# Row normalisation of three layer norms moved from VectorE to GpSimd in a one-core decoder layer

## The chip, the cores and the metric

One NeuronCore of a Trainium2 chip runs the whole kernel. The metric is the time of one execution on the device in microseconds (us); lower is better.

## What is computed

A decoder layer over 4 batches of 512 tokens with 512 columns: gated linear attention with 16 heads, attention on a context, and a feed-forward part with quantised weights and a Hadamard transform. Behind each of the three the result is added to the row and the row is normalised, without weight or bias:

```python
def _layernorm(x, axis=-1, eps=1e-05):
    m = jnp.mean(x, axis=axis, keepdims=True)
    v = jnp.var(x, axis=axis, keepdims=True)
    return (x - m) / jnp.sqrt(v + eps)

x = _layernorm(x + _L0_attn_ref(x, ...), axis=-1)
x = _layernorm(x + _L0_xattn_ref(x, ctx_1024, ...), axis=-1)
x = _layernorm(x + _L0_ffn_ref(x, ...), axis=-1)
```

All inputs and the output are fp32. The feed-forward part quantises each normalised row by its largest absolute value, to 8 bits.

## The kernel before

Y (128 partitions x 16 tiles x 512 columns) holds the rows of the layer all the time: tile 4b + i has the 128 tokens i of batch b. Attention goes in 32 steps, one for a pair of heads and a batch; each step adds its share into four tiles of Y (L1236). When a batch has had its last head pair, its cross part starts, and is spread between the stages of the following steps; behind the last step ("the seam") the feed-forward part goes in 64 units of 128 hidden columns, four of them to a batch tile of the down projection.

Every engine runs its own list of instructions in order and waits on semaphores (named in `S[...]`). The lists come from one order that all engines walk through: `attention_order`, `seam_order` and `ffn_order`. Between the stages of the steps, the table `PLACES` names for each batch at which place a stage of its cross part comes (for batch 0 `centre=400, n1=406, x101=414`, for batch 3 `centre=518, n1=520, x101=524`), and the table `UNIT` does the same for the stages of a unit (`add` 35 units behind the gate matmul, `normal` 37, `low` 2). An engine that has nothing to do at a stage passes it.

The three norms, before the change:

- First norm (`n1`), four tiles at a time. Stage `centre`: VectorE takes `bn_stats` (L1240), `bn_aggr` (L1242) and adds EPS to the variance (L1244) for each tile; GpSimd raises each to the power -1/2 (`root`, L1513). Stage `n1`: VectorE normalises four tiles (`normalise`, L1249). TensorE turns the tiles in stages `x101` and `x123` (L661).
- Second norm (`n2`), tile by tile. Stage `xm0_out` to `xm3_out`: VectorE first finishes the tile before (`finish`: normalise L1249, largest absolute value L1268), adds the product into Y (L1319) and takes the moments. GpSimd takes the root. The fourth tile is finished in `x_round1`.
- Third norm (`n3`), tile by tile in stages `add` (L1424 to L1431, for the last tile L1413 to L1420) and `normal` (L1434), the root on GpSimd (L1537). Then the tile is stored.

What else these engines do there. VectorE: masks of scores (L1194, L1146), the gate product GS (L1360), the product M of gate and up (L1367), the scaling of Wo slices (L1081), the scale of attention rows XI (L1257), the rounding of rows (L1340) and of hidden rows (L1402). GpSimd: the low parts of split fp32 weights (L1491), the clamp and cast of ternary weights (L1499, L1502), the root for the gated attention output (L1509), and LO, the low part of M (L1532). M has three buffers: its product n waits until LO of product n - 3 is written (`dve.wait_ge(S["h_lo"], n - 2)`, a count). TensorE's PSUM banks are handed on in the order of a table (`HOLD`): a matmul waits until the engine that reads its bank's last content is through. TensorE's lines: L486, L489, L492 the three passes of a split fp32 product, L549 scores, L600 weights, L614 values, L591 the turn of the exponentials, L646 energies, L719 gate and up, L728 the second Hadamard pass, which reads LO.

Of the kernel before, what the change touches and what calls it, by code (L numbers as in the profile page):

```python
# [10 lines left out]
ALU = mybir.AluOpType  # L11
# [7 lines left out]
EPS = 1e-5  # L19
# [221 lines left out]
def build(nc, x, xT, Wq, Wk, Wv, Wg, Ws, Wo, gw, cT, xWqT, xbq, xWkT, xbk, wgT, wuT, wdT, cst, out):  # L241
    with ExitStack() as top:
# [12 lines left out]
        Y = sb("Y", [128, 16, 512])  # L255
# [813 lines left out]
        def vector(engine):  # L1069
# [168 lines left out]
            def centre(name, k, i):  # L1238
# [4 lines left out]
                dve.wait_ge(S[name + "_moments"], 2 * k + 2)  # L1243
                engine.tensor_scalar(rs[:, i:i + 1], mv[:, i, 1:2], EPS, None, ALU.add).then_inc(S[name + "_var"], 1)  # L1244

            def normalise(name, k, i):
                y = Y[:, k, :]
                dve.wait_ge(S[name + "_rstd"], k + 1)
                engine.tensor_scalar(y, y, mv[:, i, 0:1], rs[:, i:i + 1], ALU.subtract,  # L1249
                                     ALU.mult).then_inc(S[name + "_applied"], 1)  # L1250
# [14 lines left out]
            def finish(b, i):  # L1265
                normalise("n2", 4 * b + i, i)
# [4 lines left out]
            def cross(stage, b):  # L1271
# [11 lines left out]
                elif stage == "n1":  # L1283
                    for i in range(4):
                        normalise("n1", 4 * b + i, i)
# [27 lines left out]
                elif stage in ("xm0_out", "xm1_out", "xm2_out", "xm3_out"):  # L1313
# [7 lines left out]
                    centre("n2", 4 * b + i, i)  # L1321
                elif stage in ("x_round0", "x_round1"):
# [30 lines left out]
            def ffn(stage, n):  # L1353
# [19 lines left out]
                elif stage in ("scale", "clamp", "turn_q_out", "add", "normal"):  # L1373
                    ffn_tile(stage, n)

            def ffn_tile(stage, i):
# [32 lines left out]
                elif stage == "add" and i == 15:  # L1409
# [7 lines left out]
                    dve.wait_ge(S["n3_moments"], 32)  # L1417
                    engine.bn_aggr(mv3[:, k, :], st3[:]).then_inc(S["n3_moments"], 1)
                    dve.wait_ge(S["n3_moments"], 33)
                    engine.tensor_scalar(rs3[:, k:k + 1], mv3[:, k, 1:2], EPS, None, ALU.add).then_inc(S["n3_var"], 1)  # L1420
                elif stage == "add":
# [6 lines left out]
                    dve.wait_ge(S["n3_moments"], 2 * i + 1)  # L1428
                    engine.bn_aggr(mv3[:, k, :], st3[:, k, :]).then_inc(S["n3_moments"], 1)
                    dve.wait_ge(S["n3_moments"], 2 * i + 2)  # L1430
                    engine.tensor_scalar(rs3[:, k:k + 1], mv3[:, k, 1:2], EPS, None, ALU.add).then_inc(S["n3_var"], 1)  # L1431
                elif stage == "normal":
                    dve.wait_ge(S["n3_rstd"], i + 1)
                    engine.tensor_scalar(y, y, mv3[:, k, 0:1], rs3[:, k:k + 1], ALU.subtract,  # L1434
                                         ALU.mult).then_inc(S["n3_applied"], 1)
# [44 lines left out]
        def gpsimd(engine):  # L1480
# [30 lines left out]
            def root(name, k, i):  # L1511
                pool.wait_ge(S[name + "_var"], k + 1)
                engine.tensor_tensor(rs[:, i:i + 1], rs[:, i:i + 1], half[:, 0:1], ALU.pow).then_inc(S[name + "_rstd"], 1)  # L1513

            def cross(stage, b):
# [4 lines left out]
                elif stage == "centre":  # L1520
                    for i in range(4):
                        root("n1", 4 * b + i, i)
# [227 lines left out]
```

## Time and profile before

| | us |
|---|---|
| three runs | 1487.88, 1489.14, 1489.43 |
| median | 1489.14 |
| the profiled execution | 1489.89 |
| its span, first to last instruction | 1488.1 |
| TensorE matmul busy in it | 1449.3 |
| VectorE busy | 1090.8 |
| ScalarE busy | 639.2 |
| GpSimd busy | 435.8 |

The engines are PE (TensorE, its weight loads PEld), DVE (VectorE), ACT (ScalarE), POOL (GpSimd) and SP (SyncE). A busy time says how long an engine worked, not whether anyone waited for it. The span is some 1.8 us shorter than the time of the same execution. A row in brackets `[1.57 <-DVE M L1367]` says that the engine stood idle for that long before the instruction, and which instruction ended the wait.

### The profile page before, as it was taken

The page shows a single profiled execution, that of the slowest core. Times are in us where ns is not written, and L with a number is a line of the kernel's source. Part 1 is how long each engine was busy: PE and PEld are TensorE (multiplying, and loading weights), DVE is VectorE, ACT ScalarE, POOL GpSimd, SP SyncE. Part 2 cuts the span into 40 slices and gives each one's busy share as a digit, 9 for nine tenths or more (in the row PEclk, how much of TensorE's full clock was granted, in tenths as well). Part 3 has the DMA queues.
Part 4 walks back from the last instruction along what each step waited for, and adds up shares of the span by engine and source line. Part 5 has one row for each costly group of instructions (what it writes and reads, how often), then busy time and mean ns, then how long its engine had stood idle before and what let it go on. Part 6 is the DMA issues. An engine that isn't in the chain of part 4 may idle for free.

```text
span 1488.1 us, 23933 instructions
## 1 busy us (share of the span) xinstructions
PE 1449.3 (97%) x9206; PEld 1170.7 (79%) x9240; DVE 1090.8 (73%) x2060; ACT 639.2 (43%) x1205; POOL 435.8 (29%) x282
## 2 busy tenths in 40 slices
PE   8999999999999999999999999999999898999998
PEld 6888888888888888888888888878888555666675
DVE  5567766676667777776677687687787786977788
ACT  4333333333323333333434334234343457776775
POOL 0311011211205455435454423221421343333320
PEclk9999999999999999999999999999999999999999
DMA  5545433443524454445655311101211125344552
GB/s 157 176 133 132 119 97 103 124 118 95 152 69 136 118 141 127 132 110 134 171 155 160 112 43 51 51 7 36 79 43 49 73 79 184 114 135 140 158 172 91
DMA packets 213297, 166.53 MB, mean 112 GB/s; under 512 B 89664, under 2 KB 174528, under 8 KB 213184
## 3 DMA queue, kind: packets, MB, share of 16 engines
q1 hardware_dynamic: 191920, 133.27, 30.5%
q10 hardware_dynamic: 21264, 31.73, 7.1%
q8 instruction: 74, 1.21, 0.4%
q14 instruction: 39, 0.32, 0.1%
HBM read 115.02 MB, written 49.94 MB: 111 GB/s over the span
## 4 chain that ended last, share of the span: by engine, by line
PE 86%; DVE 7%; DMA 2%; ACT 2%; POOL 2%; issue 1%; SPq 0%; POOLq 0%; ACTq 0%; DVEq 0%
PE bank L486 17%; PE bank L492 17%; PE bank L489 17%; PE bank L719 7%; PE bank L614 4%; PE bank L734 4%; PE bank L755 3%; PE bank L576 2%; PE bank L549 2%; PE bank L600 2%; DVE AM L1194 1%; PE bank L571 1%; PE bank L557 1%; PE bank L584 1%; DVE OKM L1172 1%
## 5 line engine op out<-in xcount | busy, mean ns | idle before, releaser
L486 PE MATMUL bank<-Wh,X 128*128 128x512 f32 x512 | 205.6, 402 | 0.1
L492 PE MATMUL bank<-Wh,X 128*128 128x512 f32 x512 | 200.0, 391 | 0.0
L489 PE MATMUL bank<-Wl,X 128*128 128x512 f32 x512 | 199.3, 389 | 0.0
L486 PE MATMUL bank<-X,Wh 128*128 128x512 f32 x384 | 156.7, 408 | 6.3 <-ACT Wh L812 6.3
L1491 POOL TENSOR_TENSOR Wl<-RAW,Wh 128x512 fp32r<-128x512 f32 (+1 forms) x65 | 112.1, 1735 | 136.8 <-ACT Wh L812 136.6
L492 PE MATMUL bank<-X,Wl 128*128 128x512 f32 x384 | 151.2, 394 | 0.0
L489 PE MATMUL bank<-X,Wh 128*128 128x512 f32 x384 | 150.6, 392 | 0.0
L1509 POOL TENSOR_TENSOR sm<-sm,half 128x8 f32<-128x8 f32 x32 | 52.7, 1648 | 331.9 <-DVE sm L1201 331.9
L1532 POOL TENSOR_TENSOR LO<-M,HI 128x512 fp32r<-128x512 f32 x64 | 82.7, 1292 | 161.7 <-PE bank L728 131.6
L874 ACT ACTIVATE V<-bank 128x256 f32<-128x256 f32 x128 | 49.0, 383 | 183.0 <-PE bank L492 182.8
L719 PE MATMUL bank<-XT,W 128*128 128x512 bf16 x492 | 119.3, 383 | 1.2 <-issue 0.2
L1499 POOL TENSOR_SCALAR RAW<-RAW 128x1024 f32<-128x1024 f32 x24 | 88.7, 3696 | 92.3 <-ACT RAW L835 90.2
L492 PEld LDWEIGHTS bank<-Wh,X 128*128 128x128 f32 x512 | 96.1, 188 | 20.9
L489 PEld LDWEIGHTS bank<-Wl,X 128*128 128x128 f32 x512 | 96.4, 188 | 18.0
L912 ACT ACTIVATE OG<-bank 128x512 f32<-128x512 f32 x64 | 38.3, 599 | 168.3 <-PE bank L614 168.3
L486 PEld LDWEIGHTS bank<-Wh,X 128*128 128x128 f32 x512 | 96.3, 188 | 18.0 <-ACT Kt L882 0.4
L1136 DVE RECIPROCAL ZT<-ZT 128x512 f32<-128x512 f32 x32 | 107.3, 3353 | 1.1
L486 PE MATMUL bank<-Woh,OTh 128*128 128x512 f32 x256 | 99.9, 390 | 0.0
L489 PE MATMUL bank<-Wol,OTh 128*128 128x512 f32 x256 | 99.6, 389 | 0.0
L492 PE MATMUL bank<-Woh,OTl 128*128 128x512 f32 x256 | 99.6, 389 | 0.0
L1172 DVE TENSOR_TENSOR OKM<-bank,ZT 128x512 f32<-128x512 f32 x32 | 22.1, 691 | 96.5 <-PE bank L576 96.4
L719 PEld LDWEIGHTS bank<-XT,W 128*128 128x128 bf16 x512 | 49.1, 99 | 53.4 <-issue 5.8
(219 smaller groups left out, 3282.0 us busy)
## 6 DMA issues: line engine op xcount, KB each, us to landing
z_scratch<-EV SPq DMA_DIRECT2D x64, 256.0 KB, 2.1
Z<-z_scratch SPq DMA_DIRECT2D x16, 1024.0 KB, 5.8
o_scratch<-OG ACTq DMA_DIRECT2D x96, 128.0 KB, 2.4
AM<-o_scratch ACTq DMA_DIRECT2D x24, 512.0 KB, 4.6
RAW<-wgT SPq DMA_DIRECT2D x16, 512.0 KB, 4.6
RAW<-wuT SPq DMA_DIRECT2D x16, 512.0 KB, 4.3
RAW<-wdT SPq DMA_DIRECT2D x16, 512.0 KB, 4.4
RAW<-Wo SPq DMA_DIRECT2D x14, 512.0 KB, 4.4
```

Source lines behind the costliest of these rows:

```text
L486: engine.matmul(o, lh(c), rh(c), start=c == 0, stop=False)
L489: engine.matmul(o, lh(c), rl(c), start=False, stop=False)
L492: last = engine.matmul(o, ll(c), rh(c), start=False, stop=c == n - 1)
L614: mm = engine.matmul(bo[h][:, 128 * i:128 * i + 128], AM[:, h, i, :], V[:, par, i, 128 * h:128 * h + 128], start=False, stop=i == 3)
L719: mm = engine.matmul(bk[:], w[:, c, 128 * j:128 * j + 128], XT[b % 3][:, c, :], start=c == 0, stop=c == 3)
L734: mm = engine.matmul(bh[:, 128 * c:128 * c + 128], Z[:, i % 2, 4 * q + c, :], C[:, 4, :], start=True, stop=True)
L874: engine.activation(V[:, par, i, :], bk[:, 0:256], ACT.Copy).then_inc(S["v_evac"], 1)
L1136: engine.reciprocal(ZT[:], ZT[:]).then_inc(S["z_recip"], 1)
L1491: engine.tensor_tensor(lo, r, hi, ALU.subtract).then_inc(S["w_lo_g"], 1)
L1499: engine.tensor_scalar(r, r, MAGIC - 1.0, MAGIC + 1.0, ALU.max, ALU.min).then_inc(S["w3_clip"], 1)
L1509: engine.tensor_tensor(smv[:, 4, :], smv[:, 3, :], half[:, 0:8], ALU.pow).then_inc(S["o_rstd"], 1)
L1532: engine.tensor_tensor(LO[:, n % 2, :], M[n % 3], HI[:, n % 3, :], ALU.subtract).then_inc(S["h_lo"], 1)
```

## The change

The normalise instruction goes to GpSimd's list for all three norms, with the same operands and at the same stage; for the second norm it follows the root of its tile at once. In the first norm VectorE adds EPS to the four variances of a batch in one instruction and GpSimd takes their four roots in one. In the third norm VectorE's `bn_aggr` waits until the normalise of the tile two before has been done, since it writes the same mean.

```diff
@@ vector @@
                 engine.bn_aggr(mv[:, i, :], st[:, i, :]).then_inc(S[name + "_moments"], 1)
-                dve.wait_ge(S[name + "_moments"], 2 * k + 2)
-                engine.tensor_scalar(rs[:, i:i + 1], mv[:, i, 1:2], EPS, None, ALU.add).then_inc(S[name + "_var"], 1)
-
-            def normalise(name, k, i):
-                y = Y[:, k, :]
-                dve.wait_ge(S[name + "_rstd"], k + 1)
-                engine.tensor_scalar(y, y, mv[:, i, 0:1], rs[:, i:i + 1], ALU.subtract,
-                                     ALU.mult).then_inc(S[name + "_applied"], 1)
+
+            def variances(name, k, i, tiles=1):
+                dve.wait_ge(S[name + "_moments"], 2 * (k + tiles))
+                engine.tensor_scalar(rs[:, i:i + tiles], mv[:, i:i + tiles, 1], EPS, None,
+                                     ALU.add).then_inc(S[name + "_var"], tiles)
             def finish(b, i):
-                normalise("n2", 4 * b + i, i)
                 dve.wait_ge(S["n2_applied"], 4 * b + i + 1)
                     for i in range(4):
                         centre("n1", 4 * b + i, i)
-                elif stage == "n1":
-                    for i in range(4):
-                        normalise("n1", 4 * b + i, i)
+                    variances("n1", 4 * b, 0, 4)
                     centre("n2", 4 * b + i, i)
+                    variances("n2", 4 * b + i, i)
                     dve.wait_ge(S["n3_moments"], 2 * i + 1)
+                    dve.wait_ge(S["n3_applied"], i - 1)
                     engine.bn_aggr(mv3[:, k, :], st3[:, k, :]).then_inc(S["n3_moments"], 1)
-                elif stage == "normal":
-                    dve.wait_ge(S["n3_rstd"], i + 1)
-                    engine.tensor_scalar(y, y, mv3[:, k, 0:1], rs3[:, k:k + 1], ALU.subtract,
-                                         ALU.mult).then_inc(S["n3_applied"], 1)
@@ gpsimd @@
-            def root(name, k, i):
-                pool.wait_ge(S[name + "_var"], k + 1)
-                engine.tensor_tensor(rs[:, i:i + 1], rs[:, i:i + 1], half[:, 0:1], ALU.pow).then_inc(S[name + "_rstd"], 1)
+            def root(name, k, i, tiles=1):
+
+                pool.wait_ge(S[name + "_var"], k + tiles)
+                engine.tensor_tensor(rs[:, i:i + tiles], rs[:, i:i + tiles], half[:, 0:tiles],
+                                     ALU.pow).then_inc(S[name + "_rstd"], tiles)
+
+            def normalise(name, k, i):
+                y = Y[:, k, :]
+                pool.wait_ge(S[name + "_rstd"], k + 1)
+                engine.tensor_scalar(y, y, mv[:, i, 0:1], rs[:, i:i + 1], ALU.subtract,
+                                     ALU.mult).then_inc(S[name + "_applied"], 1)
                 elif stage == "centre":
+                    root("n1", 4 * b, 0, 4)
+                elif stage == "n1":
                     for i in range(4):
-                        root("n1", 4 * b + i, i)
+                        normalise("n1", 4 * b + i, i)
                 elif stage in ("xm0_out", "xm1_out", "xm2_out", "xm3_out"):
                     root("n2", 4 * b + i, i)
+                    normalise("n2", 4 * b + i, i)
+                elif stage == "normal":
+                    y = Y[:, n, :]
+                    pool.wait_ge(S["n3_rstd"], n + 1)
+                    engine.tensor_scalar(y, y, mv3[:, k, 0:1], rs3[:, k:k + 1], ALU.subtract,
+                                         ALU.mult).then_inc(S["n3_applied"], 1)
```

The last tile's `bn_aggr` has the same new wait. Where the instructions come to stand on each engine, first on VectorE in the second norm of batch 0. Before:

```order
L1319 TENSOR_TENSOR Y<-Y,bank 128x512
L1240 BN_STATS st<-Y 128x6
L1242 BN_AGGR mv<-st 128x2
L1244 TENSOR_SCALAR rs<-mv 128x1
L1172 TENSOR_TENSOR OKM<-bank,ZT 128x512
L1249 TENSOR_SCALAR Y<-Y,mv,rs 128x512
L1268 TENSOR_REDUCE ax<-Y 128x1
L1319 TENSOR_TENSOR Y<-Y,bank 128x512
```

and now (L1313 is L1319, L1246 is L1244, L1264 is L1268):

```order
L1313 TENSOR_TENSOR Y<-Y,bank 128x512
L1240 BN_STATS st<-Y 128x6
L1242 BN_AGGR mv<-st 128x2
L1246 TENSOR_SCALAR rs<-mv 128x1
L1172 TENSOR_TENSOR OKM<-bank,ZT 128x512
L1264 TENSOR_REDUCE ax<-Y 128x1
L1313 TENSOR_TENSOR Y<-Y,bank 128x512
```

The normalise between the variance and the largest absolute value is gone from VectorE; everything else keeps its turn. On GpSimd, from the last root of attention on (the first norm of batch 3, in the feed-forward part; `sm` is the root L1509, `LO` the low part), before:

```order
L1509 TENSOR_TENSOR sm<-sm,half 128x8
L1532 TENSOR_TENSOR LO<-M,HI 128x512 x8
L1513 TENSOR_TENSOR rs<-rs,half 128x1 x4
L1532 TENSOR_TENSOR LO<-M,HI 128x512 x12
L1513 TENSOR_TENSOR rs<-rs,half 128x1
```

and now:

```order
L1502 TENSOR_TENSOR sm<-sm,half 128x8
L1537 TENSOR_TENSOR LO<-M,HI 128x512 x8
L1507 TENSOR_TENSOR rs<-rs,half 128x4
L1537 TENSOR_TENSOR LO<-M,HI 128x512 x2
L1513 TENSOR_SCALAR Y<-Y,mv,rs 128x512 x4
L1537 TENSOR_TENSOR LO<-M,HI 128x512 x10
L1507 TENSOR_TENSOR rs<-rs,half 128x1
```

The four roots are one instruction, and the four normalises stand between the second and the third of the low parts that follow it. In the first norm of batch 2 they stand ahead of `sm` in the same way; in batches 0 and 1 behind it.

## Rows read from the trace of the kernel before

**Rows 1.** The page, busy time: us (share of the span) xinstructions of each engine.
```profile
PE 1449.3 (97%) x9206; PEld 1170.7 (79%) x9240; DVE 1090.8 (73%) x2060; ACT 639.2 (43%) x1205; POOL 435.8 (29%) x282
```

**Rows 2.** Stretches: us, busy us of each engine, granted clock, DMA share, GB/s.
```profile
1310.00:1440.00 130.00, 129.21 (x815) 86.08 (x829) 101.84 (x206) 93.96 (x148) 41.26 (x37) 1.00 0.48 149
```

**Rows 3.** Waits of TensorE, 870 to 1310 us: total us, times, longest.
```profile
PE bank L614 <- DVE AM L1194: 3.3, 2, 2.1
PE bank L646 <- DVE M L1367: 1.6, 1, 1.6
...
PE bank L600 <- DVE Y L1236: 0.6, 1, 0.6
PE bank L591 <- ACT OKN L905: 0.4, 1, 0.4
```

**Rows 4.** Groups of GpSimd by shape: xcount | busy us, mean ns | idle before.
```profile
L1499 POOL TENSOR_SCALAR RAW<-RAW 128x1024 f32<-128x1024 f32 x24 | 88.7, 3696 | 92.3 <-ACT RAW L835 90.2 <-DMA w_scratch<-BW 2.1
L1532 POOL TENSOR_TENSOR LO<-M,HI 128x512 fp32r<-128x512 f32 x64 | 82.7, 1292 | 161.7 <-PE bank L728 131.6 <-ACT HI L1001 30.1
...
L1491 POOL TENSOR_TENSOR Wol<-RAW,Woh 128x1024 fp32r<-128x1024 f32 x13 | 30.8, 2371 | 157.8 <-ACT Woh L812 157.8
L1502 POOL TENSOR_SCALAR BW<-RAW 128x1024 bf16<-128x1024 f32 x24 | 26.2, 1093 | 2.0
```

**Rows 5.** VectorE in order of time, 974 to 988: start us, us, instruction.
```profile
975.66 0.54 DVE L1249 TENSOR_SCALAR Y<-Y,mv,rs 128x512 f32<-128x512 f32 x1
976.23 0.69 DVE L1268 TENSOR_REDUCE ax<-Y 128x1 f32<-128x512 f32 x1
...
986.21 0.55 DVE L1249 TENSOR_SCALAR Y<-Y,mv,rs 128x512 f32<-128x512 f32 x1
```

**Rows 6.** GpSimd, then VectorE, in order of time, 1054 to 1066.
```profile
1054.22 4.95 POOL L1491 TENSOR_TENSOR Wl<-RAW,Wh 128x1024 fp32r<-128x1024 f32 x2 [1.43 <-ACT Wh L812]
...
1060.85 0.69 DVE L1268 TENSOR_REDUCE ax<-Y 128x1 f32<-128x512 f32 x1
...
1064.04 1.48 DVE L1249 TENSOR_SCALAR Y<-Y,mv,rs 128x512 f32<-128x512 f32 x1 [0.65 <-POOL rs L1513]
1065.56 0.69 DVE L1268 TENSOR_REDUCE ax<-Y 128x1 f32<-128x512 f32 x1
```

**Rows 7.** Groups of VectorE: the addition of EPS in norms 1 and 2.
```profile
L1244 DVE TENSOR_SCALAR rs<-mv 128x1 f32<-128x1 f32 x32 | 4.9, 154 | 1.1
```

**Rows 8.** VectorE, GpSimd and TensorE in order of time, 1216 to 1225.
```profile
1216.88 3.86 DVE L1249 TENSOR_SCALAR Y<-Y,mv,rs 128x512 f32<-128x512 f32 x4
1220.66 0.68 DVE L1367 TENSOR_TENSOR M<-bank,GS 128x512 f32<-128x512 f32 x1
...
1224.63 0.69 DVE L1367 TENSOR_TENSOR M<-bank,GS 128x512 f32<-128x512 f32 x1 [0.70 <-ACT GS L1004]
...
1216.73 1.27 POOL L1532 TENSOR_TENSOR LO<-M,HI 128x512 fp32r<-128x512 f32 x1 [1.14 <-ACT HI L1001]
...
1221.40 0.50 PE L646 MATMUL bank<-W 128*128 128x512 f32 x1 [1.57 <-DVE M L1367]
```

**Rows 9.** VectorE, the last compute instruction of the kernel.
```profile
1485.08 0.55 DVE L1434 TENSOR_SCALAR Y<-Y,mv,rs 128x512 f32<-128x512 f32 x1 [0.66 <-POOL rs L1537]
```

**Rows 10.** GpSimd, the root of the gated output behind the first norm of batch 2.
```profile
1095.58 1.66 POOL L1509 TENSOR_TENSOR sm<-sm,half 128x8 f32<-128x8 f32 x1 [4.41 <-DVE sm L1201]
```

**Rows 11.** Stretches of 4 us; the granted clock is the third figure from the end.
```profile
992.00:996.00 4.00, 2.02 (x12) 2.02 (x13) 3.03 (x7) 2.37 (x5) 3.60 (x2) 0.84 0.02 7
996.00:1000.00 4.00, 4.00 (x21) 3.69 (x20) 3.76 (x12) 1.73 (x4) 3.18 (x6) 0.73 0.20 59
...
1220.00:1224.00 4.00, 2.50 (x9) 1.53 (x9) 3.23 (x6) 1.67 (x4) 0.32 (x2) 1.00 0.01 4
```

**Rows 12.** VectorE, then GpSimd, in order of time, 1293 to 1296.
```profile
1294.18 1.50 DVE L1249 TENSOR_SCALAR Y<-Y,mv,rs 128x512 f32<-128x512 f32 x1
...
1293.91 1.48 POOL L1532 TENSOR_TENSOR LO<-M,HI 128x512 fp32r<-128x512 f32 x1 [0.73 <-ACT HI L1001]
```

More of the change, by code:

```diff
@@ L1372, in ffn @@
                                          apply_absolute_value=True).then_inc(S["h_absmax"], 1)
-                elif stage in ("scale", "clamp", "turn_q_out", "add", "normal"):
+                elif stage in ("scale", "clamp", "turn_q_out", "add"):
                     ffn_tile(stage, n)
@@ L1428, in ffn_tile @@
                     dve.wait_ge(S["n3_moments"], 2 * i + 1)
+                    dve.wait_ge(S["n3_applied"], i - 1)
                     engine.bn_aggr(mv3[:, k, :], st3[:, k, :]).then_inc(S["n3_moments"], 1)
@@ L1525, in cross @@
                     root("n2", 4 * b + i, i)
+                    normalise("n2", 4 * b + i, i)
             def ffn(stage, n):
+                k = n % 2
                 if stage == "low":
@@ L1534, in ffn @@
                 elif stage == "add":
-                    k = n % 2
                     pool.wait_ge(S["n3_var"], n + 1)
```

## Prediction

> **What bounds the kernel now.** I read the busy shares first, then the stretches, then who waits for whom on TensorE, and last the order of time around each of those waits. The busy shares [rows 1] say that TensorE works 97% of the span and VectorE 73%; GpSimd works 29%. So neither the VectorE time that the change frees (48 row tiles at 0.54 us and more) nor the GpSimd time that it adds is worth anything by itself. Only the moments count at which TensorE stands still for one of them. From 1310 to 1440 us there are none to speak of: TensorE is busy 129.21 of 130 us [rows 2], and half of the third norm's tiles lie there. The waits of TensorE from 870 to 1310 us, where the first two norms are, give the places [rows 3]: 3.3 us before L614 in two waits (2.1 and 1.2), 1.6 before L646, 0.6 before L600, 0.4 before L591. In front of each, VectorE has a row of instructions without a gap, and L1249, the normalise of norms 1 and 2, stands in three of them. The second point is the very end, where everything is serial. All other normalises have TensorE work over them.
>
> **The change, part by part.** Call T the time of one GpSimd normalise of 128x512. The trace has no such instruction. GpSimd's one-tensor operation with two arithmetic steps (L1502, 128x1024, add and multiply) takes 1093 ns; its clamp (L1499, max and min, same size) takes 3696 ns [rows 4]. The fixed part comes from the two-tensor subtractions, 1292 ns for 512 columns (L1532) and 2371 for 1024 (the Wol form of L1491): 1079 ns for 512 columns, so about 0.2 us fixed. Hence T is 0.2 + (1.09 - 0.2)/2 = 0.65 us by the add-and-multiply row and 0.2 + (3.70 - 0.2)/2 = 1.95 us by the clamp. Subtract and multiply are arithmetic of the first kind, so I take the nearer row, with a little for the two per-partition operands: T = 0.7; both ends stay for the range. The Trainium skill, "GPSIMD Engine Reference", section 3.1, says that a body of up to two operations runs at 1.03 cycles per element, and its section 7 that bodies which compare and select run at about 2.03. From its 1.2 GHz the estimate is 0.44 us plus the fixed part, and the sum would be the one below. The ratio of the two rows agrees in direction. The same page's section 4.1 speaks against the change: elementwise work belongs on VectorE.
>
> *Place 1, 974 to 994 us (second norm of batch 0).* VectorE runs without a gap from 974.3 to 991.8, and two normalises lie in it. Each costs from its start to the start of the next instruction: 975.66 to 976.23, 0.57 us, and the one from 986.21 on the same within 0.01, together 1.15 us [rows 5]. Their GpSimd versions are finished long before, since GpSimd is idle there. What follows (four adds into Y, the scaling of a Wo slice, ScalarE's copy of it, then the mask L1194) is the chain that TensorE's 0.6 and 2.1 us waits hang on [rows 3]. Gain 1.15.
>
> *Place 2, 1055 to 1074 us (second norm of batch 1).* Here GpSimd's queue comes into play: the root, then the normalise, then weight work, and the absmax L1268 on VectorE waits for it. Tile 2 before: VectorE waits 0.65 us for the root, normalises from 1064.04 (1.48 us, as GpSimd was at work) and starts the absmax at 1065.56 [rows 6]. Now the absmax can start at 1064.0 + T = 1064.7, earlier by 0.8. The wait of 0.4 before L591 [rows 3] goes: gain 0.4. With T = 1.95 it turns round: tile 1's root can't start before two weight subtractions end at 1059.2, so its absmax, 1060.85 in the trace, would start at 1059.2 + 0.5 + 1.95 = 1061.6, 0.8 late; tile 2's statistics come 0.8 later with it, and its absmax at 1064.0 + 0.8 + 1.95 = 1066.7, 1.2 after the 1065.56 of before: a loss of about 1.1.
>
> *Place 3, 1086 to 1091 us (first norm of batch 2).* The four variance additions (154 ns each [rows 7]) become one. The next instruction starts before an addition ends, so I take half of 3 x 0.154: 0.2 us off the second wait of L614. Nothing, or 0.46, are the ends.
>
> *Place 4, 1216 to 1232 us (first norm of batch 3).* Four normalises take VectorE from 1216.88 to 1220.66, and the product M (L1367) behind them frees the bank for which L646 waits 1.57 us [rows 8]. They go: M can start about 3 us earlier, and the wait disappears: gain 1.6. But on GpSimd the four now stand ahead of a low part LO (L1532), as the excerpt of the order shows. The LO before them ends at 1216.73 + 1.27 = 1218.0; the delayed one ends at 1218.0 + 4T + 1.28. The third M behind the normalises, 1224.63 in the trace, waits for this LO, because they share a buffer of three. TensorE needs it at 1224.63 - 1.57 = 1223.1. So four normalises are covered up to T = 0.94, and each microsecond of T beyond costs 4 us. With 0.7 the LO ends at 1222.1: covered. With 1.95 it costs 4.0, a net loss of 2.4.
>
> *The end.* The last normalise, 0.55 us from 1485.08 on, after a wait for the root [rows 9], becomes T behind that root on one engine: loss 0.15 (1.4 with T = 1.95). Nothing covers it; the last store follows.
>
> *At nothing:* the other first norms (batches 0 and 1 have several microseconds of queue before TensorE turns the tiles), the third norm's first fifteen tiles (TensorE's gate matmuls until 1472, ScalarE's rounding of H behind that), the new wait of bn_aggr for the tile two before (some 16 us earlier on GpSimd), and GpSimd's root of the gated output (L1509), which batch 2's four normalises now precede: GpSimd stood idle for 4.41 us in front of it [rows 10], and they fill 2.8 of them. Beyond T = 1.1 this root, and VectorE's gating behind it, come late.
>
> Sum: -1.15 - 0.4 - 0.2 - 1.6 + 0.15 = **-3.2 us**. The rows are from an execution of 1489.89 us, whose span is 1488.1; it would come to 1486.7. The median of the runs shown is 0.75 us lower, and against it the forecast is 1489.14 - 3.2 = **1485.9 us**.
>
> **Rivals.** *A, the clock comes back.* Behind the waits of place 1 TensorE's granted clock falls, from 2.4 GHz towards its 1.2 GHz level: 0.84 in 992 to 996 and 0.73 in 996 to 1000, a loss of (0.16 + 0.27) x 4 = 1.7 us of work. In 1220 to 1224, around the wait of 1.57 us, it stayed 1.00 [rows 11]. The two waits of place 1 are 2.66 us in all before and 1.5 after. If that keeps the clock up, another 1.7 us go: 1489.14 - 4.9 = **1484.2 us**. For it: 1.5 is below the wait that did no harm. Against: two waits lie together, with small matmuls between.
>
> *B, GpSimd takes twice VectorE's time,* T = 1.1: place 2 gives 0, place 4 costs 0.6 of its 1.6, the end 0.55. -1.15 - 0.2 - 1.0 + 0.55 = -1.8: **1487.3 us**.
>
> *C, slower: GpSimd takes the clamp's pace.* T = 1.95: -1.15 - 0.2 + 1.1 + 2.4 + 1.4 = +3.55: **1492.7 us**. The mechanism is place 4: the LO waits behind four normalises and holds M, and with it gate banks. It decides from T = 1.4 on, where -1.15 - 0.2 + 0.3 - 1.6 + 4 x 0.46 + 0.85 is zero. Against it: the add-and-multiply row is a third of the clamp's. For it: that row has immediate operands and writes bf16, and this one has neither.
>
> *D, the two engines block each other.* A VectorE normalise that began at 1294.18, while GpSimd's LO ran (1293.91 to 1295.39), took 1.50 us instead of 0.54: it ended only after the LO [rows 12]. The Trainium skill, "SBUF — State Buffer", section "SBUF: two separate sides", calls this an exclusive lock, held for a whole instruction; by it the rounding of XI (L1340), the scale of attention rows (L1257) and the clamp of HQ (L1402) could each lose up to T beside a normalise. At places 1 and 4 none of them stands beside one, and near the end the clamps at 1476 come after it, so I give it no more than one such meeting on the path, 1.50 - 0.54 = 0.96 us, so 1486.9: inside the forecast's own spread.
>
> **Numbers.** A measurement of this kernel can tell about 0.2%, 3 us, from no change. Chances: forecast 0.34 (D is in it), A 0.26, B 0.12, C 0.24, something in the order of the queues that I do not see 0.04. The forecast lies just beyond the 3 us: 0.20 of it counts as faster, 0.14 as same. A: 0.23 faster, 0.03 same. B: 0.12 same. C: 0.14 slower, 0.10 same, since T anywhere from 1.4 to 1.9 ends within 3 us. The rest: slower. Faster 0.43, same 0.39, slower 0.18. The range reaches from A less 0.8 us for the later waits of place 4 (1483.4) to C (1492.7).
>
> **What would show it.** T itself, in the new GpSimd group. Place 1: the waits of L600 and L614 at 1.5 us together, and the granted clock of the next 8 us. Place 4: no wait before the second L646; the LO behind the four normalises ending before its M wants to start. The end: from the last root to the last store, T. I am wrong if T is above 0.94, if TensorE's waits before 1310 don't shrink by 3 us, or if a wait of TensorE on LO or on L1268's followers appears that was not there.

## The result, and the profile after

The changed kernel takes 1498.20 us, median of four runs (1495.94 to 1500.40); the kernel before, in the runs beside them, 1488.88 us (1487.88 to 1489.43). The ratio is 1.0063, 95% interval 1.0045 to 1.0081: 9.3 us slower. The forecast was 3.2 us faster, and its range ended at 1492.7. The profiled execution took 1499.42 us, its span 1497.6.

The busy times [rows 1], in the profile after:

```profile
PE 1452.5 (97%) x9240; PEld 1169.6 (78%) x9240; DVE 1066.8 (71%) x2000; ACT 638.2 (43%) x1205; POOL 537.6 (36%) x318
```

VectorE lost 24.0 us of work and GpSimd gained 101.8. The gain stands in two new groups of GpSimd by shape (count | busy us, mean ns | idle before), 106.7 us together; the roots taken four at once save some 5. L1513 is the normalise of norms 1 and 2, L1546 that of norm 3:

```profile
L1513 POOL TENSOR_SCALAR Y<-Y,mv,rs 128x512 f32<-128x512 f32 x32 | 66.3, 2079 | 1.8
L1546 POOL TENSOR_SCALAR Y<-Y,mv,rs 128x512 f32<-128x512 f32 x16 | 40.4, 2525 | 0.8
```

T is 2.08 us, three times the 0.7 that the sum was made with, and above its upper end of 1.95. Now the waits of TensorE from 870 to 1310 us, which answer to [rows 3]:

```profile
PE bank L726 <- DVE M L1362: 4.2, 1, 4.2
PE bank L624 <- DVE OG L1215: 4.0, 1, 4.0
PE bank L614 <- DVE AM L1194: 2.9, 3, 1.8
PE bank L591 <- ACT OKN L905: 2.8, 1, 2.8
PE bank L486 <- DVE OG L1215: 2.0, 1, 2.0
...
PE bank L486 <- POOL W L1520: 1.2, 1, 1.2
```

The 4.0 for L624 was there before. The 4.2 is place 4, the 2.8 place 2, and the 2.0 and the 1.2 stand at places that the sum had at nothing or did not name.

**Reading where the time went.** The profiled executions stand up to 2.3 us apart at an instruction that comes before anything that the change touches (the first row below), so ends don't compare. I took instructions of ScalarE that both kernels have once per step or tile, and noted how many microseconds later each one starts than in the kernel before. A change from one landmark to the next is what that stretch cost. The first landmark lies ahead of everything that was changed. The columns are the changed kernel and five kernels of the experiments below.

| landmark (its start before) | after | n1_back | n2_back | spread3 | n2b0 | add_mult |
|---|---|---|---|---|---|---|
| X1h L935 (865.5) | +0.8 | -0.8 | +0.3 | +0.4 | +1.5 | -0.1 |
| ET L868 (972.7) | +1.2 | -0.7 | +0.6 | +0.9 | +1.6 | -0.7 |
| OTh L922 (1067.1) | -1.2 | -3.0 | +0.6 | -1.4 | -0.8 | -2.3 |
| XT L989 (1086.4) | +2.8 | -0.5 | +0.6 | +1.2 | -0.8 | -2.9 |
| ET L868 (1116.8) | +5.1 | -1.0 | +2.8 | +3.5 | -1.3 | -3.3 |
| OTh L922 (1185.6) | +6.5 | +0.5 | +2.7 | +4.9 | -1.3 | -3.3 |
| XT L989 (1208.3) | +5.4 | -0.6 | +3.0 | +3.8 | -2.1 | -4.2 |
| H L1023 (1276.2) | +8.0 | -1.0 | +5.5 | +3.6 | -2.7 | -6.5 |
| H L1023 (1475.1) | +7.9 | -0.5 | +5.8 | +3.3 | -2.4 | -7.1 |
| end of the span (1488.1) | +9.5 | +1.1 | +7.3 | +4.9 | -2.4 | -5.8 |

Down the first column: place 1 gives back 2.3 us; then +4.0 at place 2, +2.3 at the first norm of batch 2, +1.4 before 1185, -1.1 up to 1208 (n1_back, n2b0 and add_mult have it too: the granted clock of 1180 to 1200 was 0.91 in them and 0.83 before; but spread23, below, with all 48 normalises on GpSimd, had 0.83 again, so the change is not shown to earn it), +2.6 at place 4, nothing in the whole stretch of the feed-forward part, +1.6 at the end.

**How a slow instruction gets onto the path.** GpSimd, batch 2 of the first norm, in order of time, and the VectorE instruction that waits:

```profile
1094.21 8.25 POOL L1513 TENSOR_SCALAR Y<-Y,mv,rs 128x512 f32<-128x512 f32 x4
1102.43 1.67 POOL L1502 TENSOR_TENSOR sm<-sm,half 128x8 f32<-128x8 f32 x1
```

```profile
1104.13 2.16 DVE L1215 SCALAR_TENSOR_TENSOR OG<-bank,sm,U 128x128 f32<-128x128 f32 x8 [5.22 <-POOL sm L1502]
```

The root L1502 has a 4.41 us gap before it in [rows 10]. Now four normalises fill 8.25 us, the root runs directly behind them, VectorE waits 5.22 us for it, and TensorE 2.0 for VectorE.

Place 4 is the same story with LO in the root's place. GpSimd, then VectorE's product M, and then TensorE:

```profile
1223.06 8.26 POOL L1513 TENSOR_SCALAR Y<-Y,mv,rs 128x512 f32<-128x512 f32 x4
1231.29 2.49 POOL L1537 TENSOR_TENSOR LO<-M,HI 128x512 fp32r<-128x512 f32 x2
```

```profile
1232.68 0.69 DVE L1362 TENSOR_TENSOR M<-bank,GS 128x512 f32<-128x512 f32 x1 [6.67 <-POOL LO L1537]
```

```profile
1233.43 0.80 PE L726 MATMUL bank<-HI,H 128*128 128x512 f32 x1 [4.19 <-DVE M L1362]
```

**The clock after a wait.** Stretches of 4 us (granted clock third from the end), which answer to [rows 11]; the first two are place 1, the third place 2, the last place 4:

```profile
992.00:996.00 4.00, 2.24 (x21) 2.14 (x20) 3.14 (x8) 2.35 (x6) 3.71 (x2) 1.00 0.03 7
996.00:1000.00 4.00, 3.65 (x20) 2.92 (x19) 3.79 (x10) 1.42 (x3) 2.73 (x3) 1.00 0.20 60
1074.00:1078.00 4.00, 2.69 (x9) 2.33 (x10) 3.06 (x7) 1.54 (x4) 1.80 (x1) 0.62 0.48 149
1232.00:1236.00 4.00, 2.57 (x6) 1.13 (x7) 3.32 (x6) 1.97 (x3) 2.98 (x3) 0.50 0.00 0
```

Place 1 kept 2.4 GHz here (one kernel of the experiments, add_mult_n12, lost it there). Behind the new waits of 2.8 and 4.2 us TensorE ran at the lower level of 1.2 GHz (0.50) for some microseconds: its bf16 group of eight, L719, took 3.64 us there instead of 1.89.

### The profile page after: what moved, and what is told of

It reads as the page before. It is cut to its first block, busy times and chain, and to the rows that moved or that the text cites. A ratio compares the mean times of both kernels' runs of the same rounds, so it can differ in the third digit from the quotient of the medians.

```text
span 1497.6 us, 23965 instructions
## 1 busy us (share of the span) xinstructions
PE 1452.5 (97%) x9240; PEld 1169.6 (78%) x9240; DVE 1066.8 (71%) x2000; ACT 638.2 (43%) x1205; POOL 537.6 (36%) x318
## 4 chain that ended last, share of the span: by engine, by line
PE 81%; DVE 7%; POOL 5%; DMA 3%; ACT 2%; issue 1%; SPq 0%; POOLq 0%; ACTq 0%; DVEq 0%
PE bank L486 17%; PE bank L492 16%; PE bank L489 16%; PE bank L719 6%; PE bank L614 4%; PE bank L734 3%; PE bank L755 3%; PE bank L576 2%; POOL Y L1513 2%; PE bank L549 2%; PE bank L600 2%; DVE AM L1194 1%; PE bank L571 1%; PE bank L557 1%; PE bank L584 1%
## 5 line engine op out<-in xcount | busy, mean ns | idle before, releaser
L1502 POOL TENSOR_TENSOR sm<-sm,half 128x8 f32<-128x8 f32 x32 | 52.8, 1652 | 321.9 <-DVE sm L1201 321.9
L719 PE MATMUL bank<-XT,W 128*128 128x512 bf16 x512 | 124.2, 387 | 0.0
L719 PEld LDWEIGHTS bank<-XT,W 128*128 128x128 bf16 x512 | 49.4, 100 | 54.6 <-issue 7.8
```

Of the source, the lines that this page charges most:

```text
L719: mm = engine.matmul(bk[:], w[:, c, 128 * j:128 * j + 128], XT[b % 3][:, c, :], start=c == 0, stop=c == 3)
L1502: engine.tensor_tensor(smv[:, 4, :], smv[:, 3, :], half[:, 0:8], ALU.pow).then_inc(S["o_rstd"], 1)
```

## Experiments

Three theories. **Q**: a normalise takes 2.08 us on GpSimd, and what stands behind it in GpSimd's order comes late at a few places. **L**: the two engines hinder each other when they work at once, at each of the 48. **K**: the clock falls by chance. All kernels were timed beside the kernel before, which had medians of 1488.55 to 1489.16 us. The expectations of the first group count the changed kernel as 1498.2.

**1. Each norm back on VectorE, then all three.** The edit of n1_back:

```diff
+                elif stage == "n1":
+                    for i in range(4):
+                        normalise("n1", 4 * b + i, i)
```

on VectorE, with GpSimd's own branch dropped; n2_back and n3_back do the same for `finish` and for the stage `normal`, batch_only for all three.

> The changed kernel with the first norm's normalises back on VectorE (its one sum of four variances and its one root of four stay); second and third norm stay on GpSimd. Theory Q (each normalise takes 2.08 us on GpSimd, and the loss is what stands in GpSimd's order behind it at a few places): the first norm costs about 2.0 us at batch 2 (the root for the heads' output waits behind four normalises) and 2.6 us at batch 3 (LO waits behind four normalises), so the time falls by about 4.5 us from 1498.2 to about 1493.7, VectorE's wait of 6.67 us for LO near 1226 is gone, and the root of sm near 1102 comes back under its producer. Theory L (normalises on GpSimd slow VectorE wherever they run beside it, equally for each of the 48): a third of the 9.3 us comes back, 1495.1. Theory K (the loss is TensorE's clock dropping at random places): no fall that goes with the edit, 1496 to 1500.

> The changed kernel with the second norm's normalises back on VectorE; first and third on GpSimd. Theory Q: of the second norm, batch 0 gains about 1.8 us on GpSimd (with the clock that no longer falls near 994), batch 1 loses about 2.9 us (the wait of 2.8 us before L591 near 1073 and the half clock behind it), batch 2 about 1.3 us (the low part of W behind a normalise near 1168); so undoing it gives back 2.4 us: about 1495.8, with the wait before L591 at 0.4 us again and the low clock near 996 back. Theory L: a third of the loss, 1495.1. Theory K: 1496 to 1500, whatever is undone.

> The changed kernel with the third norm's normalises back on VectorE; first and second on GpSimd. Theory Q: only the last tile's 2.08 us in place of 0.55 us counts, 1.5 us: about 1496.7, and the stretch 1310 to 1440 takes as long as before although its GpSimd normalises were 3.04 us each. Theory L: the sixteen normalises of this norm are the ones that meet VectorE's clamp (3.04 us instead of 2.08), so here the most would come back: 3.1 us or more, 1495.1 or lower. Theory K: 1496 to 1500.

> All three norms' normalises back on VectorE: what is left of the change is that a batch's four variances of the first norm get their small number in one instruction, and their roots are one GpSimd instruction of four columns. Theory Q: the three saved VectorE instructions a batch free 0.5 us before AM near 1091, of which I forecast 0.2 us on the path; 1488.4 to 1488.9 against 1488.9 before, no difference that can be measured. Theory L: the same. A rival R: the batched root starts only when the fourth variance is there and ends later by about 0.5 us than the fourth root did, and the normalise behind it waits: 0 to 1 us slower.

| kernel | median us (runs) | against before, 95% |
|---|---|---|
| n1_back | 1492.65 (1490.95 to 1495.81) | 1.0027 [1.0017, 1.0038] |
| n2_back | 1497.24 (1494.99 to 1499.56) | 1.0053 [1.0041, 1.0066] |
| n3_back | 1498.63 (1496.11 to 1498.80) | 1.0062 [1.0048, 1.0075] |
| batch_only | 1489.57 (1487.25 to 1491.23) | 1.0004 [0.9996, 1.0013] |

The three norms don't share the loss equally: 5.5, 1.0 and none, so L as stated falls. K falls too as the cause of the 9.3 us: the waits of TensorE follow the edits exactly. n1_back has no wait for OG and none of 4.2 for M, and keeps the 2.8 of place 2; n2_back is the reverse:

```profile
PE bank L591 <- ACT OKN L905: 2.8, 1, 2.8
...
PE bank L726 <- DVE M L1371: 0.8, 1, 0.8
```

(n1_back) and

```profile
PE bank L726 <- DVE M L1370: 4.2, 1, 4.2
...
PE bank L486 <- DVE OG L1215: 2.0, 1, 2.0
...
PE bank L591 <- ACT OKN L905: 0.4, 1, 0.4
```

(n2_back). Two of my sizes failed. n2_back gave 1.0 instead of 2.4 and n3_back nothing instead of 1.5, though its profile shows no loss at the end (1475 to the end: 0.0 instead of 1.6). The executions of one kernel with long waits lie 2.7 to 4.9 us apart, and those of the kernel before 1.5 to 3.3, so differences of 1.5 us can't be read from medians of four or five; they can from the landmarks. The batching alone makes no difference that can be measured.

**2. Order alone, and placement alone.** spread3 moves batch 3's four normalises in GpSimd's order and nothing else:

```diff
                 elif stage == "n1":
-                    for i in range(4):
+                    for i in range(4 if b < 3 else 0):
                         normalise("n1", 4 * b + i, i)
...
                     ffn(stage, n)
+                    if stage == "low" and S_LOW[0] is not None:
+                        S_LOW[0] += 1
+                        for i in SPREAD.get(S_LOW[0], ()):
+                            normalise("n1", 12 + i, i)
```

(S_LOW counts the LOs from batch 3's root on; SPREAD is {1: (0,), 3: (1, 2), 5: (3,)}.) n2b0 puts only the second norm of batch 0 on GpSimd (`if b in (0,)` there, `if b not in (0,)` on VectorE), and the other 44 normalises on VectorE; best1 adds batch 3 of the first norm, spread as above.

> The changed kernel with one thing moved: GpSimd's four normalises of the first norm's last batch no longer stand in a block ahead of two LOs, but one behind the first LO after the root, two behind the third, one behind the fifth. All 48 normalises stay on GpSimd at 2.08 us each. Theory Q (the loss is the block that holds LO back): the 2.6 us of this place come back, and the 3.86 us that VectorE no longer spends on them may give up to the 1.6 us that I had forecast: 1494.0 to 1495.6 against 1498.2, VectorE's wait of 6.67 us for LO gone. Theory L (GpSimd's work slows VectorE wherever it stands): no change, 1498. A third, D: the GpSimd queue is full in this stretch in any order, and LO comes late in smaller parts: 1497 to 1498.

> Only those normalises on GpSimd that the trace shows to gain there: the second norm's of batch 0, and the first norm's of batch 3, spread between the LOs as in spread3; the other 40 on VectorE; variances and roots of four together. Theory Q: 1488.6 less 1.9 to 2.3 us at batch 0 less up to 1.6 us at batch 3: 1484.7 to 1485.7, faster than both kernels. Theory L: eight normalises on GpSimd cost 8 x 0.19 us, 1490.1. Theory K (clock drops at random): 1488 to 1490.

> Only the second norm's four normalises of batch 0 on GpSimd; the other 44 on VectorE; variances and roots of four together. Theory Q: GpSimd's idle time there takes them, AM comes about 1.1 us earlier and the clock does not fall near 994: 1.9 to 2.3 us faster than the kernel with all on VectorE (1489.6, and 1488.6 for the kernel before), so 1486.5 to 1487.5. Theory K: the clock falls there or not by chance: 1488.5 to 1489.5 in the median.

| kernel | median us (runs) | against before, 95% |
|---|---|---|
| spread3 | 1494.36 (1493.88 to 1496.86) | 1.0045 [1.0033, 1.0058] |
| best1 | 1485.67 (1484.80 to 1486.87) | 0.9983 [0.9974, 0.9992] |
| n2b0 | 1485.01 (1484.68 to 1487.52) | 0.9981 [0.9972, 0.9990] |

spread3 runs the same 48 normalises on the same engine and is 3.8 us faster than the change, as Q expected: between 1208 and 1276 it loses nothing (-0.3 in the table), where the block lost 2.6. That is what the block costs. But the 1.6 us that the forecast added there did not come. The wait before L646 is gone in spread3 and best1, while their clock from 1215 to 1240 is 0.93; n2b0, which still waits 1.0 us there, has 1.00. best1's stretch:

```profile
1215.00:1240.00 25.00, 21.37 (x103) 12.55 (x102) 17.12 (x31) 19.19 (x36) 15.47 (x11) 0.93 0.35 116
```

and n2b0's:

```profile
1215.00:1240.00 25.00, 20.25 (x102) 11.86 (x100) 18.97 (x34) 18.87 (x36) 8.31 (x8) 1.00 0.35 117
```

0.07 of 25 us is 1.75 us: as much as the wait. But the wait does not decide it: batch_only, which has the wait of 1.0 as well, shows 0.93. best1's median lies where it was expected, but the part expected of batch 3 did not come (0.5 us of up to 1.6 between 1208 and 1276, and no gain over n2b0). n2b0 beats the kernel before with four tiles on GpSimd, by 3.5 us in the medians (4.6 against batch_only, timed in another group); its interval, 1.5 to 4.2 us, holds the 1.9 to 2.3 expected, and between 972.7 and 1067.1 its profile gains 2.3.

spread23 adds the same cure for batch 2: two normalises ahead of the root for the heads' output, two behind.

```diff
-                    for i in range(4 if b < 3 else 0):
+                    for i in range((4, 4, 2, 0)[b]):
...
                     engine.tensor_tensor(smv[:, 4, :], smv[:, 3, :], half[:, 0:8], ALU.pow).then_inc(S["o_rstd"], 1)
+                    if HELD[0]:
+                        HELD[0] = False
+                        for i in (2, 3):
+                            normalise("n1", 8 + i, i)
```

(HELD is set when the first two are done.)

> As spread3 (all 48 normalises on GpSimd at 2.08 us each, batch 3's four spread between LOs), and of batch 2's four normalises of the first norm two now stand ahead of the root for the heads' output and two behind it. Theory Q: in the changed kernel's profile that root could have run from about 1097.8 and ran at 1102.43 behind the four; now it starts at about 1098.4, so TensorE's wait of 2.0 us for OG goes, while the transposes of Y (L661) wait until the fourth normalise ends, about 1.6 us instead of 0.3 us: about 0.7 us faster than spread3, 1493.7 against 1494.4, with more if the clock stays up. Theory L (working at once is what costs): 1494.4, unchanged.

It took 1494.34 us (1492.48 to 1495.41), ratio 1.0037 [1.0024, 1.0051]: no faster than spread3. The wait for OG is gone and another has its place:

```profile
PE bank L661 <- POOL Y L1519: 1.9, 1, 1.9
```

From 1086 to 1117 the profile shows 0.6 us less lost than in spread3 (1.7 against 2.3), the direction and size of theory Q but below what medians tell. This place is full: root and four normalises don't fit, in either of the two orders tried.

spread23 has batch 3's normalises where spread3 has them, and no wait before L646 either. Its stretch shows a clock of 1.00:

```profile
1215.00:1240.00 25.00, 22.70 (x110) 12.50 (x108) 19.45 (x37) 19.11 (x36) 19.29 (x13) 1.00 0.29 94
```

and from 1208 to 1276 it gains 1.9 us where spread3, at 0.93, gained 0.3. So the 1.6 us were there to be had at T = 2.08 as well, in an execution in which the clock stayed up. Its total does not show them, because the same profile lost 1.6 us more than spread3's behind the wait before L591 (clock 0.93 from 1066 to 1090, 1.00 in spread3) and 1.3 from 1185 to 1208 (0.83 against 0.91).

**3. What sets T.** Two kernels write each of the 16 tiles of the first norm with another form of instruction and were read for durations only.

> A look at durations alone. The 16 row tiles of the first norm are each written by another form of GpSimd instruction on 128x512 float32 in place (the output is then not the reference's): both scalars read from a tile (the form of the change), one of them, none; subtract, add, mult, max and min; a tensor_tensor add; a copy; one of 128x256. Theory P (a scalar read from a tile makes it slow, the nearest rows were wrong because theirs are numbers in the instruction): 2.08 us with two from a tile, about 1.4 with one, 0.55 to 0.7 with none. Theory O (subtract is the slow operation): 2.08 us wherever subtract stands, 0.55 with add and mult whichever way the scalars come. Theory M (the price per element is the price of GpSimd for any operation but a few): 1.9 to 2.1 us for most forms, and 1.05 us for 128x256.

> A second look at durations alone, as in forms, on 128x512 float32 in place (the output is not the reference's). From the first: subtract then mult 2.08 us with both scalars from a tile and 1.93 with both in the instruction, max then min 1.93, one operation alone 1.51 to 1.57, but mult then add 1.14 and 0.62, add then mult 0.77 and 0.62. Theory F (only add and mult together, in either order, have a fast form): mult then mult, add then add, add then max and add then subtract about 1.9 to 2.1 us, mult then subtract 2.0, add then mult with two scalars from a tile 0.77 again, and half of that plus a fixed part for 128x256. Theory S (it is subtract, max and min that are slow, add and mult fast in any pair): mult then mult and add then add 0.6 to 0.8 us.

The first four of forms, and three of forms2, as GpSimd ran them:

```profile
886.60 2.09 POOL L1514 TENSOR_SCALAR Y<-Y,mv,rs 128x512 f32<-128x512 f32 x1
888.68 1.57 POOL L1516 TENSOR_SCALAR Y<-Y,mv 128x512 f32<-128x512 f32 x1
890.24 1.57 POOL L1518 TENSOR_SCALAR Y<-Y,rs 128x512 f32<-128x512 f32 x1
891.79 1.14 POOL L1520 TENSOR_SCALAR Y<-Y,rs,mv 128x512 f32<-128x512 f32 x1
```

```profile
999.65 0.78 POOL L1522 TENSOR_SCALAR Y<-Y,mv,rs 128x512 f32<-128x512 f32 x1
...
1001.76 0.78 POOL L1528 TENSOR_SCALAR Y<-Y,rs,mv 128x512 f32<-128x512 f32 x1
...
1221.63 0.56 POOL L1540 TENSOR_SCALAR Y<-Y,mv,rs 128x256 f32<-128x256 f32 x1
```

All of them, 128x512 unless said, one instruction each:

| operations | both scalars from a tile | one | none |
|---|---|---|---|
| subtract, mult | 2.08 | 2.00 | 1.93 |
| add, mult | 0.77, 0.78 | 0.70, 0.71 | 0.62 |
| mult, add | 0.78 (1.14 beside VectorE's scan) | | 0.62 |
| mult, mult | | | 0.64 |
| add, add | | | 1.95 |
| add, max; max, min; mult, subtract | | | 1.94; 1.93; 1.95 |
| add, subtract | 2.09 | | |
| one operation alone: subtract, mult, add | | 1.57, 1.57, not tried | 1.50, 1.51, 1.51 |
| 128x256: subtract, mult; add, mult | 1.23; 0.56 | | |

A copy took 0.61, a two-tensor add, subtract or mult 1.04 to 1.05. P, O, M, F and S are all wrong as stated. Three pairs are fast (add with mult in either order, mult with mult); every other pair tried, and one operation alone, takes 1.5 to 2.1. (Mult then subtract with both from a tile took 3.10, beside VectorE's scan.) Where the scalars come from is worth 0.15 us. A scalar from a tile was my worry; the operation was the price.

**4. The same normalise in the fast form.** VectorE negates the means, GpSimd adds and multiplies; the value is the same. Order and engine are those of the change; VectorE has one small instruction more for each group of variances, and GpSimd waits for it too.

```diff
+                engine.tensor_scalar(mv[:, i:i + tiles, 0], mv[:, i:i + tiles, 0], -1.0, None,
+                                     ALU.mult).then_inc(S[name + "_moments"], tiles)
...
-                engine.tensor_scalar(y, y, mv[:, i, 0:1], rs[:, i:i + 1], ALU.subtract,
+                engine.tensor_scalar(y, y, mv[:, i, 0:1], rs[:, i:i + 1], ALU.add,
                                      ALU.mult).then_inc(S[name + "_applied"], 1)
```

> The changed kernel with another form of the same normalise on GpSimd, for all three norms: VectorE negates the means (one instruction of 0.15 us behind each instruction on the variances, beside GpSimd's root), and GpSimd adds the negated mean and multiplies by the root, which took 0.77 us in the run of forms, instead of 2.08 us. Order, waits and the engine of every normalise stay those of the change. Theory Q (the price of one normalise, through the queue, made the loss): my prediction's sum was made at 0.7 us, so it should now hold: 1485.9, and 1486 to 1487.2 if the 1.6 us of batch 3 of the first norm don't come (the kernel best1 showed at most 0.4 us of them); no wait of TensorE of 2.8 us before L591, of 2.0 us for OG behind batch 2, or of 4.2 us for M. Theory L (what costs is that GpSimd and VectorE work at once): some of the 9.6 us stays, by 0.77 of 2.08: 1492. Theory K: 1489 to 1498.

> As add_mult for the first and second norm; the third norm's 16 normalises back on VectorE (subtract and mult, as in the kernel before). Theory Q: the end costs 0.2 us less than in add_mult, all else the same: within 0.5 us of it. Theory L: the third norm's normalises are those beside VectorE's clamps, so 1 us or more comes back.

| kernel | median us (runs) | against before, 95% |
|---|---|---|
| add_mult | 1486.67 (1484.06 to 1488.31) | 0.9984 [0.9975, 0.9993] |
| add_mult_n12 | 1484.98 (1484.38 to 1487.43) | 0.9975 [0.9966, 0.9984] |

The one word and its small helper are worth 11.5 us, and turn the change from 9.3 us slower into 2.5 faster. No wait before L591, none for OG behind batch 2, none of 4.2 for M; place 4 in add_mult, with the LOs 3.03 us behind instead of 8.26:

```profile
1213.42 3.03 POOL L1521 TENSOR_SCALAR Y<-Y,mv,rs 128x512 f32<-128x512 f32 x4
1216.41 2.53 POOL L1545 TENSOR_TENSOR LO<-M,HI 128x512 fp32r<-128x512 f32 x2
```

add_mult_n12 has the lowest median of the study, 4.2 us under the kernel before timed beside it; n2b0's, 1485.01, can't be told from it. It is 1.7 us faster than add_mult in the medians, where Q said up to 0.5; their intervals against the kernel before overlap. The clock goes with it: add_mult's executions had a mean clock of 0.995 or 0.996 except the profiled one (0.998), add_mult_n12's 0.996 to 0.998. What takes add_mult's clock down in most of its runs stays open. In the two profiles add_mult loses 1.3 us from 1475 to the end and add_mult_n12 nothing; 0.3 of it is the normalise on GpSimd, and 1.0 lies behind it: the span ends 3.4 us after the last normalise, with only the last store between, where it ended 2.4 us after it in the other profiles looked at. That is one execution.

Between these two profiles lies the cleanest look at the clock of place 4, since both run the same instructions there. The stretch in add_mult, and then in add_mult_n12:

```profile
1215.00:1240.00 25.00, 21.42 (x112) 12.85 (x111) 17.27 (x32) 20.09 (x39) 11.38 (x10) 1.00 0.45 144
```

```profile
1215.00:1240.00 25.00, 21.42 (x104) 13.15 (x103) 16.71 (x31) 19.28 (x37) 10.33 (x9) 0.93 0.38 123
```

The same busy time, 1.00 against 0.93, and from the XT of 1208 to the H of 1276 add_mult gains 1.7 us more (2.3 against 0.6).

The same two profiles differ in the same way at place 1. Both have the wait of 1.8 us before L614 and none before L600, but add_mult's clock stays at 1.00 from 992 to 1000 and add_mult_n12's does not:

```profile
992.00:996.00 4.00, 3.81 (x20) 3.82 (x21) 3.79 (x10) 1.12 (x3) 3.29 (x2) 0.60 0.23 66
```

Between 972.7 and 1067.1 add_mult_n12 gains 0.6 us and add_mult 1.6. So theory K is wrong for the 9.3 us, but right for a part of what comes behind a wait: at places 1 and 4 the clock falls in some executions and not in others.

## Why the prediction was wrong

**The step that failed is the choice of T**: "Subtract and multiply are arithmetic of the first kind, so I take the nearer row". The row was add and multiply. Add and multiply with both scalars from a tile takes 0.77 us, so 0.7 was the right price of another instruction; subtract and multiply takes 2.08, with the clamp's kind. Of the two reasons that I gave against the row (numbers in the instruction, bf16 output) the first is worth 0.15 us, and the second nothing that shows: with numbers and fp32 output the pair took 0.62, against 0.65 worked out from the bf16 row. The upper end fell 0.13 short for just that reason: the clamp's scalars are numbers. The Trainium skill, "GPSIMD Engine Reference", section 3.1, gives one rate for bodies of up to two operations. For add and mult this holds (an estimate from its 1.03 cycles at 1.2 GHz and 0.2 us fixed is 0.64 us, measured 0.62); for subtract, max, min, add with add, and for one operation alone, the runs show 1.5 to 1.95, and the measurement decides.

**At T = 0.77 the sum holds in the total, with luck in its parts.** add_mult is the prediction's kernel at that price: 1485.9 forecast, 1486.67 measured. But its profiled execution, the fastest of its eleven, gains 5.7 us from the first landmark to the end: 1.6 at place 1, 0.6 at place 2, 0.4 at place 3, 0.9 before 1208, 2.3 at place 4 and 0.6 in the feed-forward part, less 1.3 at the end. The forecast of 3.2 lies between this and the median's 2.5.

**At T = 2.08 the sum is not the right one.** Its own terms give -1.15 + 1.4 - 0.2 + 3.0 + 1.5, some 4.5 us slower, half of the 9.3 measured. Term by term, landmarks of the change:

- *Place 1*: forecast -1.15, measured -2.3. VectorE's part came: its mask L1194 starts 1.26 us earlier against the landmark. TensorE's wait of 0.6 is gone and that of 2.1 is 1.8, but a wait of 0.4 for GpSimd's low part of X1h is new. The rest is rival A, worth the 1.7 it named: the clock stayed at 1.00. n2b0 shows place 1 alone. Of the eleven profiles with this norm of batch 0 on GpSimd ten kept the clock there and add_mult_n12's did not; the three with it on VectorE all lost it.
- *Place 2*: forecast -0.4, or +1.1 at T = 1.95; measured +4.0 in this profile and 2.6 in n1_back's and spread3's. The queue's part is as worked out: tile 2's absmax came 1.5 us late (0.4 after the 1065.56 of [rows 6], in an execution that stands 1.2 us earlier there):

```profile
1065.93 0.69 DVE L1264 TENSOR_REDUCE ax<-Y 128x1 f32<-128x512 f32 x1 [2.87 <-POOL Y L1513]
```

  Two things were not in it. Rival D's blocking struck here, on instructions that it had not named. VectorE has two-column instructions of 0.16 and 0.21 us in the profile before (L1323 and L1328 in the changed kernel):

```profile
1070.21 0.16 DVE L1328 TENSOR_SCALAR ax<-ax 128x2 f32<-128x2 f32 x1
...
1070.48 0.21 DVE L1333 TENSOR_SCALAR ax<-ax,ws 128x2 f32<-128x2 f32 x1
```

  and in the changed kernel:

```profile
1070.58 0.61 DVE L1323 TENSOR_SCALAR ax<-ax 128x2 f32<-128x2 f32 x1
...
1071.31 1.16 DVE L1328 TENSOR_SCALAR ax<-ax,ws 128x2 f32<-128x2 f32 x1
```

  and GpSimd meanwhile:

```profile
1069.09 2.08 POOL L1513 TENSOR_SCALAR Y<-Y,mv,rs 128x512 f32<-128x512 f32 x1
1071.14 1.30 POOL L1484 TENSOR_TENSOR Wl<-RAW,Wh 128x512 fp32r<-128x512 f32 x1
```

  The first ends at 1071.19, with the normalise (1071.17), the second at 1071.31 + 1.16 = 1072.47, with the weight work (1072.44): 1.4 us, read from this trace and not isolated by a run. The second thing is the half clock behind the wait: it makes the 4.0 of this profile out of the 2.6 of the profiles in which the clock stayed up.
- *Place 3*: forecast -0.2; batch_only's landmarks show -0.6 from 1086 to 1117, its median nothing.
- *Place 4*: forecast -1.6, or +2.4 at 1.95; measured +2.6, against +3.0 by the text's formula at 2.08. The mechanism and the point (0.94) were right. The gain of 1.6 behind it came in two of the five profiles in which the wait before L646 was gone and M was not held (add_mult and spread23, clock 1.00: 2.3 and 1.9 us); in the other three (spread3, best1, add_mult_n12) the clock was 0.93 and took as much.
- *The end*: +1.4 at 1.95 (1.5 at 2.08), measured +1.6.
- *At nothing*: the root of sm was covered to T = 1.1, as said, but rival C, which had T = 1.95, did not charge it; it cost 2.3. And one place was missing altogether: the low part of W (L1520) behind the last normalise of batch 2, for which TensorE waits 1.18 us near 1170; that stretch costs 1.4, and nothing in n2_back and add_mult. The third norm's first fifteen tiles were free, as forecast; TensorE was busy 130.00 of 130 us:

```profile
1310.00:1440.00 130.00, 130.00 (x837) 86.29 (x836) 98.07 (x199) 93.88 (x150) 67.24 (x47) 1.00 0.46 145
```

So rival C (0.24) had the sign and the mechanism, and came out 5.5 us short: GpSimd's queue held something back at four places, and it priced two of them, place 4 nearly right and place 2 at 1.1 us instead of 2.6 or more. Having named "beyond T = 1.1 this root comes late", I should have carried it into the case that assumed 1.95.

## What to carry to other kernels

The price of an instruction on GpSimd is that of its exact pair of operations: before work is moved there, measure that form, and try the equivalent one (negate and add for subtract), which here was worth 11.5 us on 48 instructions. When a slower engine takes work at a point of its order, list everything behind that point and the idle time ahead of each, and price every entry in every case of T, not only in the one that one believes. Move only what has idle time behind it: with four tiles of 48 on GpSimd, even in the slow form, n2b0 was 3.5 us faster than the kernel before (interval 1.5 to 4.2).

## What the runs showed of the hardware

- GpSimd's tensor_scalar on 128x512 float32: 0.62 to 0.78 us for add with mult in either order and mult with mult, 1.5 to 2.1 us for the other forms tried. One operation alone is slower than two fast ones (mult alone 1.51, mult and mult 0.64).
- The two engines hold each other up in both directions: place 2 above shows VectorE held, and here GpSimd is. What is added is not in proportion to the held instruction. A GpSimd normalise that starts beside VectorE's clamp of HQ takes 0.96 us longer whether it is long or short: 3.04 instead of 2.08 in the changed kernel, and 1.73 in add_mult, with 0.77 elsewhere:

```profile
1321.36 3.04 POOL L1546 TENSOR_SCALAR Y<-Y,mv,rs 128x512 f32<-128x512 f32 x1
```

```profile
1306.81 1.73 POOL L1555 TENSOR_SCALAR Y<-Y,mv,rs 128x512 f32<-128x512 f32 x1
```

- The granted clock of one stretch can differ between executions of the same instructions: 1.00 and 0.93 for 1215 to 1240 in add_mult and add_mult_n12, 1.7 us, and 1.00 and 0.79 for 992 to 1000 in the same two. Behind the wait of 4.2 us for M it fell in all three profiles read there (the changed kernel's, n2_back's, n3_back's: 0.86 from 1220 to 1245); behind the 2.8 before L591 in two of five (1066 to 1090: 0.93 in the changed kernel's and spread23's, 1.00 in n1_back's, n3_back's and spread3's).
